# Two attention-and-Mamba layers with FP4 feed-forward on one core: four dA buffers, own rings for the C products, a thinner SP queue

## The chip, the cores and the metric

The program runs on one core of one Trainium2 chip. The metric is the time of one execution on the device in microseconds (us); lower is better.

## The reference

Input x is (8, 1024, 256). Layer 0 is attention with relative positions (16 heads of 16, so 8 x 16 = 128 heads of 1024 tokens), layer 1 two Mamba layers; each is followed by a gated feed-forward on blockwise FP4 values, and all are modulated by scales and shifts made from a condition. What matters here, cut down:

```python
# attention, per head: c2p and p2c are gathered diagonally from tables of relative positions
scores = (Q K^T) * scale + c2p + p2c ; probs = softmax(scores) ; ctx = probs V
# Mamba layer, per batch; D_INNER = 512, D_STATE = 16
u  = silu(conv(xc)) ; dt = softplus(x_dbl[:RANK] @ dt_w.T + dt_b) ; A = -exp(A_log)
dA = exp(dt_t[:, :, None] * A)
h  = dA * h + (dt_t * u_t)[:, :, None] * B_t[:, None, :]     # a scan over time
y  = einsum('bdn,bn->bd', h, C_t)
y  = (y + u * Dskip) * silu(z) ; h = y @ out_w.T
x  = layer_norm(h) * ln_w + ln_b + residual
```

## The kernel before, in words

Everything is written out by hand: each engine has its own program, and semaphores tie them. Stages follow each other: modulation, attention, its output product, feed-forward, two Mamba layers (`mamba_layer`, names mb_), feed-forward. The change touches two of them.

**Attention** (`attention_loop`, from L701). A loop over 128 heads, two per turn; per head 8 tiles of 128 queries (index i). For each tile TensorE makes scores one tile ahead (L866) and adds into them, by a transposing product, a 3-block band of position terms from `skew` (L870); two position tables of the next head (`table`, L883); turns the probabilities (L899); and makes the context of the tile before (L918). VectorE adds the other band (L1018) and takes the maximum (L1020), ScalarE makes the exponentials (L971) and keeps the tables in SBUF (L966). A table reaches its skewed form through DRAM: SP stores it (`store_table`, L784, one DMA per table, 16 per head), and loads it back with a row pitch one shorter (`load_skew`, L793, four DMAs for each of four parts of two tiles). SP works its queue in order: `head` (L796) waits until the head before has done its scores, loads the next head's three operands (L771), then the two operands of the tables of the head after (L775, tile `eopnd`), then for each i two stores, at certain i the loads of a part (each waits until its tables have landed), the values (L778) and the context store (L816). Part 3 of a head (tiles 6 and 7) is loaded in the next turn of `head`, at i = 0. TensorE needs it before the scores of tile 5.

**Mamba** (`mamba_layer`). 16 items per layer (8 batches, two halves of 512 time steps each, index t.u; the second half starts its scans from `carry`). Channels are on partitions in 4 chunks, and with 16 states an item has 64 slots s. In a slot:

- ScalarE makes dA[s] = exp(dt * A) (L2198) into a ring of DA_RING = 2 banks in PSUM;
- GpSimd makes bx[s] = dtu * B (L1921) into a ring of 4 in SBUF;
- VectorE scans (L2016) dA[s] and bx[s] into `hs` (PSUM, two banks) or, if GpSimd multiplies by C, into `hs_sb` (SBUF, two);
- the product with C: VectorE (L1976), one slot later, or GpSimd (L1928), three slots later, for the 18 slots of TIMES_C_POOL; both into one ring g of 4;
- TensorE sums the products over the states into y_ps (L2159), one slot later, in the order of slots.

```python
                        nc.vector.tensor_tensor_scan(state(s), dA[:, s % DA_RING, :], bx[:, s % RINGS, :],
```

The work of the neighbouring items is laid into the slots by tables of slot numbers (the AT_ names, L1590 on): input projections, convolution, the softplus of dt (ScalarE L2177 to L2184, VectorE L2002 on v and lnp, GpSimd L1934, L1937, L1940), gating (L1983), output projection, and the norm: statistics L1987 and L1993, reciprocal root on GpSimd (L1905 to L1910), centering on ScalarE (L2188), weight and shift on VectorE (L2040, L2044), residual on GpSimd (L1952). Layer 1 also adds a base row and a gate on VectorE (L2049, L2053). SP loads B and C rows, spread over all partitions, by quarters.

Of the kernel before, what the change touches and what calls it, by code (L numbers as in the profile page):

```python
# [2333 lines left out]
```

## Time and profile before

| | |
|---|---|
| median of 3 runs | 10254.26 us (10250.23 to 10259.6) |
| the profiled execution's own time | 10262.97 us |
| its span, first to last instruction | 10261.3 us |
| busy: TensorE (PE), VectorE (DVE) | 8391.0 us (82%), 8398.0 us (82%) |
| busy: ScalarE (ACT), GpSimd (POOL) | 5633.4 us (55%), 4948.9 us (48%) |
| mean granted TensorE clock | 0.923 of full speed |
| DMA | 1498.79 MB, mean 146 GB/s |

Busy times are sums over the whole span, so an engine that is full in one stage and idle in another shows a middling share. In a group of instructions, "x" is the count, then come busy time, mean ns of one, and the idle time of the engine just before them with what ended it. A duration includes any time in which the instruction is held back after it started. In a timeline, equal instructions that follow each other are one row ("x3"), with their time together.

### The profile page before, as it was taken

How to read it: one execution, taken by the hardware profiler on the slowest of the kernel's cores; microseconds unless marked ns; L12 is line 12 of the kernel's file. 1: busy time of each engine (PE TensorE's matmuls, PEld its weight loads, DVE VectorE, ACT ScalarE, POOL GpSimd, SP SyncE). 2: the span in 40 equal slices, each digit the busy share in tenths (PEclk: the TensorE clock that was granted, in tenths of full speed). 3: DMA queues.
4: the chain of work that ended last, by engine and by line, in shares of the span. 5: the costliest groups of instructions: out<-in, count | busy, mean ns of one | idle time of the engine just before them, and what ended most of it. 6: DMA issues, size and time to landing. Idle time of an engine off the chain costs nothing. (4 is left out here: it accounts for less than half of the span.)

```text
span 10261.3 us, 177062 instructions
## 1 busy us (share of the span) xinstructions
PE 8391.0 (82%) x48396; PEld 4841.9 (47%) x48396; DVE 8398.0 (82%) x13204; ACT 5633.4 (55%) x9153; POOL 4948.9 (48%) x4685
## 2 busy tenths in 40 slices
PE   4569899989988888499688888888688888887599
PEld 2236666666666666366333333333233333333366
DVE  4558888888888887699588888888688888888799
ACT  1237777777777776133365555555455555555233
POOL 0000000000000000088488888888598888888487
PEclk7779999999999999699898998898899999999799
DMA  5578888888888888311111111111122221122111
GB/s 178 204 234 281 277 278 279 279 279 278 277 279 277 277 278 261 111 43 42 61 74 76 76 68 55 68 74 75 51 80 84 84 84 71 62 81 80 45 43 40
DMA packets 1218155, 1498.79 MB, mean 146 GB/s; under 512 B 101997, under 2 KB 1073277, under 8 KB 1185000
## 3 DMA queue, kind: packets, MB, share of 16 engines
q1 hardware_dynamic: 1217832, 1495.78, 44.7%
q14 instruction: 279, 2.29, 0.1%
q8 instruction: 44, 0.72, 0.0%
HBM read 932.33 MB, written 564.60 MB: 146 GB/s over the span
## 5 line engine op out<-in xcount | busy, mean ns | idle before, releaser
L2159 PE MATMUL mb_y_ps<-mb_g,ident 128*128 128x512 f32 x4096 | 2227.9, 654 | 589.9 <-DVE mb_g L1976 356.3
L1921 POOL TENSOR_TENSOR mb_bx<-mb_dtu,mb_bc 128x512 f32<-128x512 f32 x2048 | 2569.3, 1282 | 132.7 <-DVE mb_hs L2016 78.6
L2198 ACT ACTIVATE mb_dA<-mb_dt,mb_a_neg 128x512 f32<-128x512 f32 x2048 | 1403.7, 689 | 1854.9 <-DVE mb_hs L2016 1181.4
L1355 POOL MEMSET f_magic<- 128x1 f32 x2 | 0.2, 98 | 3842.8 <-POOLq L127 3842.8
L2159 PEld LDWEIGHTS mb_y_ps<-mb_g,ident 128*128 128x128 f32 x4096 | 789.3, 204 | 1782.9 <-issue 755.4
L966 ACT ACTIVATE at_tab<-at_e_ps 128x384 f32<-128x384 f32 x2064 | 1011.8, 490 | 968.4 <-PE at_e_ps L883 967.4
L1020 DVE TENSOR_REDUCE at_nmax<-at_s_ps 128x1 f32<-128x1024 f32 x1025 | 1255.2, 1225 | 35.2
L899 PE MATMUL at_pT_ps<-ident,at_probs 128*128 128x128 f32 x8192 | 1115.7, 280 | 140.3 <-ACT at_probs L971 131.8
L971 ACT ACTIVATE at_probs<-at_s_ps,at_nmax 128x1024 f32<-128x1024 f32 x1025 | 1140.6, 1113 | 96.2 <-DVE at_nmax L1020 77.0
L899 PEld LDWEIGHTS at_pT_ps<-ident,at_probs 128*128 128x128 f32 x8192 | 920.0, 142 | 403.3 <-ACT at_probs L971 378.1
L2016 DVE TENSOR_TENSOR_SCAN mb_hs<-mb_dA,mb_carry,mb_bx 128x512 f32<-128x512 f32 x736 | 927.7, 1280 | 204.8 <-POOL mb_bx L1921 117.2
L1976 DVE TENSOR_TENSOR mb_g<-mb_hs,mb_bc 128x512 f32<-128x512 f32 x1472 | 994.0, 675 | 69.9 <-PE mb_y_ps L2159 68.6
L2016 DVE TENSOR_TENSOR_SCAN mb_hs<-mb_dA,mb_bx 128x512 f32<-128x512 f32 x736 | 893.6, 1223 | 165.0 <-ACT mb_dA L2198 96.1
L866 PE MATMUL at_s_ps<-at_opnd 105*128 105x512 bf16 (+3 forms) x2818 | 808.8, 327 | 201.9 <-DMA at_skew<-at_tables 199.2
L1018 DVE TENSOR_TENSOR at_s_ps<-at_s_ps,at_skew 128x384 f32<-128x384 f32 (+1 forms) x1025 | 541.2, 528 | 495.6 <-PE at_s_ps L870 375.1
L1928 POOL TENSOR_TENSOR mb_g<-mb_hs_sb,mb_bc 128x512 f32<-128x512 f32 x576 | 736.5, 1279 | 312.6 <-DVE mb_hs_sb L2016 180.2
L1025 DVE COPY at_probsT<-at_pT_ps 128x512 f32<-128x512 f32 x1024 | 697.0, 681 | 0.0
L918 PE MATMUL at_c_ps<-at_probsT,at_val 128*32 128x128 f32 x16384 | 663.9, 280 | 1.6 <-ACT at_probsT L978 1.6
L870 PE MATMUL at_s_ps<-ident,at_skew 128*128 128x128 f32 x2818 | 612.9, 275 | 0.0
L2092 PE MATMUL mb_ring<-mb_xc,mb_diag 128*128 128x512 f32 x1024 | 526.8, 600 | 41.6 <-ACT mb_u L2249 39.0
L918 PEld LDWEIGHTS at_c_ps<-at_probsT,at_val 128*32 128x32 f32 x16384 | 387.4, 109 | 214.6 <-issue 203.9
L866 PEld LDWEIGHTS at_s_ps<-at_opnd 105*128 105x128 bf16 x2818 | 242.8, 98 | 435.2 <-DMA at_skew<-at_tables 223.9
(236 smaller groups left out, 14473.1 us busy)
## 6 DMA issues: line engine op xcount, KB each, us to landing
at_tables<-at_tab SPq DMA_DIRECT2D x2064, 192.0 KB, 3.5
at_skew<-at_tables SPq DMA_DIRECT2D x1030, 256.0 KB, 3.1
mb_bc<-mb_bc_rows SPq DMA_DIRECT2D x256, 1024.0 KB, 6.4
at_skew<-at_tables SPq DMA_DIRECT2D x773, 128.0 KB, 3.5
at_opnd<-at_q_st SPq DMA_DIRECT2D x129, 210.0 KB, 3.4
at_opnd<-at_kl_st SPq DMA_DIRECT2D x129, 210.0 KB, 3.9
at_opnd<-at_kr_st SPq DMA_DIRECT2D x129, 210.0 KB, 5.2
at_eopnd<-at_q_st SPq DMA_DIRECT2D x130, 192.0 KB, 4.3
```

The lines of the kernel that those rows point to most:

```text
L866: mm = nc.tensor.matmul(s_ps[:, b, a * P:z * P], opnd[:, u, 0, q], opnd[:, u, side, a * P:z * P], start=True, stop=(len(near) == 0))
L899: mm = nc.tensor.transpose(pT_ps[:, hb, k * P:(k + 1) * P], probs[:, i % 2, c:c + P], ident[:, :])
L918: mm = nc.tensor.matmul(c_ps[lane * VW:(lane + 1) * VW, q:q + P], val[:, h.u, k + lane, :], probsT[:, i0 % 2, (k + lane) * P:(k + lane + 1 ...
L966: nc.scalar.activation(tab[:, e, :], e_ps[:, 0:BAND], ACT.Copy).then_inc(s_tab, 1)
L971: nc.scalar.activation(probs[:, i % 2, :], s_ps[:, i % 2, :], ACT.Exp, bias=nmax[:, i % 2:i % 2 + 1], scale=1.0).then_inc(s_exp, 1)
L1020: nc.vector.tensor_reduce(nmax[:, b:b + 1], s_ps[:, b, :], axis=AX.X, op=ALU.max, negate=True).then_inc(s_max, 1)
L1921: pool.tensor_tensor(bx[:, s % RINGS, :], dtu[:, c, :], bc[:, 0, n, :], ALU.mult).then_inc(s_bx, 1)
L1928: pool.tensor_tensor(g[:, s1 % RINGS, :], state(s1), bc[:, 1, s1 % STATE, :], ALU.mult).then_inc(s_gp, 1)
L1976: nc.vector.tensor_tensor(g[:, s1 % RINGS, :], state(s1), bc[:, 1, n, :], ALU.mult).then_inc(s_g, 1)
L2016: nc.vector.tensor_tensor_scan(state(s), dA[:, s % DA_RING, :], bx[:, s % RINGS, :], initial=carry[:, s:s + 1] if k.u else 0.0, op0=ALU.mu ...
L2159: nc.tensor.matmul(y_ps[:, c % 2, :], ident[:, :], g[:, s1 % RINGS, :], start=False, stop=(n == STATE - 1)).then_inc(s_y, 1)
L2198: nc.scalar.activation(dA[:, s % DA_RING, :], dt[:, c, :], ACT.Exp, scale=a_neg[:, c, n:n + 1]).then_inc(s_dA, 1)
```

## The change

In attention: `eopnd` and its loads are gone, the tables are made from the first 96 rows of `opnd`, which has a semaphore for each of its three parts. One DMA stores both tables of a tile. The operands of head n + 2 are loaded at i = 6, once the scores of head n are done; the loads of a part come ahead of the store of their i.

In Mamba: DA_RING is 4, of which two buffers are in PSUM (s % 4 in 0, 1) and two in SBUF, `dA_sb` (s % 4 in 2, 3). The ring g becomes g_dve (3) and g_pool (2), each freed by TensorE's sum of the slot that used it; TensorE sums GpSimd's products 5 slots after their scan, VectorE's 1 slot after. GpSimd makes 14 C products in place of 18, and applies the output norm's weight and shift (two sums and products over 128 x 1024) in VectorE's place. The softplus steps work in dt and dtu in place of v, e and lnp, ScalarE's in two slots, GpSimd's three in three slots. Centering is done in two halves in two slots. SP waits only for the bx products before it loads B rows, and for the sums before C rows. Some slot numbers move.

The core of the diff:

```diff
-            def store_table(n1, u1, e):
-                ge(sp, s_tab, n1 * NE + e + 1)
-                part = e // 2 // (TT // len(PARTS))
-                sp.dma_start(table_dram[u1, e % 2, e // 2, 0:P, SPAN:SPAN + BAND], tab[:, e, :]).then_inc(s_tw[part], 16)
+            def store_tables(n1, u1, t):
+                ge(sp, s_tab, n1 * NE + 2 * t + 2)
+                part = [t < z for _, z in PARTS].index(True)
+                sp.dma_start(table_dram[u1, :, t, 0:P, SPAN:SPAN + BAND].rearrange("s p u -> p s u"),
+                             tab[:, 2 * t:2 * t + 2, :]).then_inc(s_tw[part], 16)
...
-                load_opnd(n + 1, 1 - u)
-                ge(sp, s_E, (n + 1) * NE)
-                load_eopnd(n + 2, u)
                 for i in range(TT):
-                    for e in range(2 * i, 2 * i + 2):
-                        store_table(n + 1, 1 - u, e)
                     for part, (_, z) in enumerate(PARTS):
-                        if z - 1 + LAG - 1 == i + 1:
+                        if z + 1 == i:
                             load_skew(n + 1, 1 - u, part)
-                        if z - 1 + LAG - 1 == i + 1 + TT:
+                        if z + 1 == i + TT:
                             load_skew(n, u, part)
-                    if i == 0:
+                    if i == TT - 2:
+                        ge(sp, s_S, n * TT + TT)
+                        load_opnd(n + 2, u)
+                    store_tables(n + 1, 1 - u, i)
+                    if i == 2:
...
-                mm = nc.tensor.matmul(e_ps[:, 0:BAND], eopnd[:, u1, side, t * P:(t + 1) * P],
+                mm = nc.tensor.matmul(e_ps[:, 0:BAND], opnd[0:ROWS, u1, side, t * P:(t + 1) * P],
...
-AT_DTK, AT_DTK_ACT = (52, 2, 15, 32), (58, 8, 21, 38)
-AT_DTK_DVE, AT_DTK_POOL = (59, 9, 22, 39), (63, 13, 26, 43)
+AT_DTK, AT_DTK_ACT = (52, 2, 15, 32), (56, 8, 21, 38)
+AT_DTK_DVE, AT_DTK_POOL = (58, 11, 23, 40), (59, 12, 24, 41)
 AT_Z, AT_Z_ACT = (40, 43, 54, 56), (46, 49, 60, 62)
 AT_U = 45
 AT_SILU_Z = 12
 AT_XDBL, AT_XDBL_ACT = 47, 53
-AT_Y = (29, 38, 54, 4)
-AT_ONORM = 26
-AT_RES = 44
-AT_OCENTER, AT_OSCALE = 34, 37
-AT_HCENTER, AT_HSCALE = 56, 59
-AT_XIN = 48
-AT_LN = 50
+AT_Y = (29, 38, 54, 7)
+AT_ONORM, AT_OCENTER, AT_OAFFINE, AT_OGATE = 26, (33, 34), (36, 38), 44
+AT_RES, AT_RES_LAST = 43, 48
+AT_XIN = 50
+AT_LN, AT_HCENTER, AT_HSCALE = 53, (58, 59), 61
 RINGS = 4
-DA_RING = 2
-
-TIMES_C_POOL = tuple(s for s in range(IC * STATE) if s * 18 // (IC * STATE) != (s + 1) * 18 // (IC * STATE))
+DA_RING, DA_PSUM = 4, 2
+G_DVE, G_POOL = 3, 2
+
+TIMES_C_POOL = tuple(s for s in range(IC * STATE) if s * 14 // (IC * STATE) != (s + 1) * 14 // (IC * STATE))
 POOL_LAG = 3
+SUM_LAG_POOL = 5
...
-        g = sb("g", [P, RINGS, BANK])
+        g_dve = sb("g_dve", [P, G_DVE, BANK])
+        g_pool = sb("g_pool", [P, G_POOL, BANK])
+        dA_sb = sb("dA_sb", [P, DA_RING - DA_PSUM, BANK])
         carry = sb("carry", [P, SLOTS])
         yz = sb("yz", [P, IC, BANK])
         o_sb = sb("o_sb", [P, QT, D])
         hs_sb = sb("hs_sb", [P, 2, BANK])
-        dA = pb("dA", [P, DA_RING, BANK])
+        dA = pb("dA", [P, DA_PSUM, BANK])
...
+        def decay(s):
+            i = s % DA_RING
+            return dA[:, i, :] if i < DA_PSUM else dA_sb[:, i - DA_PSUM, :]
...
+        def product_read(eng, t, slots, i, ring):
+
+            i = turned_over(i, ring, len(slots))
+            if i >= 0 or t.n_static != 0:
+                t = t if i >= 0 else t.plus(-1)
+                ge(eng, s_y, summed(t, slots[i]))
...
-                            sp.wait_ge(s_y, k.n * SLOTS + (IC - 1) * STATE + n + 4)
                         for i in range(2):
+                            if i == 1 and not first_body(k):
+                                at = (IC - 1) * STATE + n
+                                sp.wait_ge(s_y, summed(k, max(range(at, at + 4), key=sum_order)))
...
-                            m1 = t.n * SLOTS + s1
-                            pool.wait_ge(s_scan, m1 + 1)
-                            ge(pool, s_y, m1 - RINGS + 1)
-                            pool.tensor_tensor(g[:, s1 % RINGS, :], state(s1), bc[:, 1, s1 % STATE, :],
+                            p = slots_before(s1, True)
+                            pool.wait_ge(s_scan, t.n * SLOTS + s1 + 1)
+                            product_read(pool, t, by_pool, p, G_POOL)
+                            pool.tensor_tensor(g_pool[:, p % G_POOL, :], state(s1), bc[:, 1, s1 % STATE, :],
                                                ALU.mult).then_inc(s_gp, 1)
...
+                    if tail and s == AT_OAFFINE[0]:
+                        t = k.plus(-1)
+                        pool.wait_ge(s_ocen, t.n * 2 + 2)
+                        pool.tensor_tensor(o_sb[:, :, :], o_sb[:, :, :], ln[:, 0:1, :].to_broadcast([P, QT, D]),
+                                           ALU.mult).then_inc(s_oaff, 1)
+                    if tail and s == AT_OAFFINE[1]:
+                        pool.wait_ge(s_oaff, k.plus(-1).n * 2 + 1)
+                        pool.tensor_tensor(o_sb[:, :, :], o_sb[:, :, :], ln[:, 1:2, :].to_broadcast([P, QT, D]),
+                                           ALU.add).then_inc(s_oaff, 1)
...
-                    ge(dve, s_y, m - RINGS + 1)
-                    nc.vector.tensor_tensor(g[:, s1 % RINGS, :], state(s1), bc[:, 1, n, :], ALU.mult).then_inc(s_g, 1)
+                    d = slots_before(s1, False)
+                    product_read(dve, t, by_dve, d, G_DVE)
+                    nc.vector.tensor_tensor(g_dve[:, d % G_DVE, :], state(s1), bc[:, 1, n, :], ALU.mult).then_inc(s_g, 1)
...
-                        nc.vector.tensor_tensor_scan(state(s), dA[:, s % DA_RING, :], bx[:, s % RINGS, :],
+                        nc.vector.tensor_tensor_scan(state(s), decay(s), bx[:, s % RINGS, :],
...
-                        if s == AT_OSCALE:
-                            dve.wait_ge(s_ocen, b.n + 1)
-                            nc.vector.tensor_tensor(o_sb[:, :, :], o_sb[:, :, :],
-                                                    ln[:, 0:1, :].to_broadcast([P, QT, D]), ALU.mult).then_inc(s_ochain, 1)
-                        if s == AT_OSCALE + 1:
-                            dve.wait_ge(s_ochain, done + 3)
-                            nc.vector.tensor_tensor(o_sb[:, :, :], o_sb[:, :, :],
-                                                    ln[:, 1:2, :].to_broadcast([P, QT, D]), ALU.add).then_inc(s_ochain, 1)
...
+                    if s >= SUM_LAG_POOL and scan or s < SUM_LAG_POOL and tail:
+                        lag = s - SUM_LAG_POOL
+                        t, s1 = (k, lag) if lag >= 0 else (b, SLOTS + lag)
...
-                        nc.scalar.activation(dA[:, s % DA_RING, :], dt[:, c, :], ACT.Exp,
+                        nc.scalar.activation(decay(s), dt[:, c, :], ACT.Exp,
```

What the diff does not show is how the instructions stand. SP's queue in attention, the end of one head and the start of the next, before:

```order
L793 DMA at_skew<-at_tables 128x2x256 x2
L793 DMA at_skew<-at_tables 128x2x128 x2
L784 DMA at_tables<-at_tab 128x384 x2
L771 DMA at_opnd<-at_q_st 105x1024
L771 DMA at_opnd<-at_kl_st 105x1024
L771 DMA at_opnd<-at_kr_st 105x1024
L775 DMA at_eopnd<-at_q_st 96x1024
L775 DMA at_eopnd<-at_kl_st 96x1024
L784 DMA at_tables<-at_tab 128x384 x2
L793 DMA at_skew<-at_tables 128x2x256 x2
L793 DMA at_skew<-at_tables 128x2x128
L793 DMA at_skew<-at_tables 128x128
```

and in the change:

```order
L778 DMA at_tables<-at_tab 128x2x384
L768 DMA at_opnd<-at_q_st 105x1024
L768 DMA at_opnd<-at_kl_st 105x1024
L768 DMA at_opnd<-at_kr_st 105x1024
L778 DMA at_tables<-at_tab 128x2x384
L788 DMA at_skew<-at_tables 128x2x256 x2
L788 DMA at_skew<-at_tables 128x2x128 x2
L778 DMA at_tables<-at_tab 128x2x384 x2
L788 DMA at_skew<-at_tables 128x2x256 x2
L788 DMA at_skew<-at_tables 128x2x128
L788 DMA at_skew<-at_tables 128x128
L778 DMA at_tables<-at_tab 128x2x384 x2
```

The five operand loads between tables and tables are gone from the start of the head; three of them stand between part 1 and the last tables.

VectorE in Mamba, a stretch of four to five slots in the first half of a batch, before (a scan is printed as SCALAR_TENSOR_TENSOR):

```order
L2016 SCALAR_TENSOR_TENSOR mb_hs<-mb_dA,mb_bx 128x512
L1973 COPY mb_carry<-mb_hs 128x1
L1976 TENSOR_TENSOR mb_g<-mb_hs,mb_bc 128x512
L2016 SCALAR_TENSOR_TENSOR mb_hs<-mb_dA,mb_bx 128x512
L1973 COPY mb_carry<-mb_hs 128x1
L1976 TENSOR_TENSOR mb_g<-mb_hs,mb_bc 128x512
L2016 SCALAR_TENSOR_TENSOR mb_hs_sb<-mb_dA,mb_bx 128x512
L1973 COPY mb_carry<-mb_hs 128x1
L1976 TENSOR_TENSOR mb_g<-mb_hs,mb_bc 128x512
L2016 SCALAR_TENSOR_TENSOR mb_hs<-mb_dA,mb_bx 128x512
L1973 COPY mb_carry<-mb_hs_sb 128x1
```

and in the change:

```order
L2076 SCALAR_TENSOR_TENSOR mb_hs_sb<-mb_dA,mb_bx 128x512
L2032 COPY mb_carry<-mb_hs 128x1
L2036 TENSOR_TENSOR mb_g_dve<-mb_hs,mb_bc 128x512
L2076 SCALAR_TENSOR_TENSOR mb_hs<-mb_dA_sb,mb_bx 128x512
L2032 COPY mb_carry<-mb_hs_sb 128x1
L2076 SCALAR_TENSOR_TENSOR mb_hs<-mb_dA_sb,mb_bx 128x512
L2032 COPY mb_carry<-mb_hs 128x1
L2036 TENSOR_TENSOR mb_g_dve<-mb_hs,mb_bc 128x512
L2076 SCALAR_TENSOR_TENSOR mb_hs<-mb_dA,mb_bx 128x512
L2032 COPY mb_carry<-mb_hs 128x1
L2036 TENSOR_TENSOR mb_g_dve<-mb_hs,mb_bc 128x512
```

The scans read `mb_dA` (PSUM) in two slots and `mb_dA_sb` (SBUF) in the next two; `mb_bx` is in SBUF throughout. All else is as before in these slots.

## Rows read from the trace of the kernel before

**Rows 1.** busy time by engine in three stretches (attention, Mamba layer 0, layer 1)
```profile
core 0: us, PE busy (x) PEld busy (x) DVE busy (x) ACT busy (x) POOL busy (x), PEclk, DMA share, GB/s
1000.00:3800.00 2800.00, 2522.00 (x28194) 1853.34 (x28193) 2280.36 (x3368) 1991.44 (x3156) 0.00 (x0) 0.99 0.88 278
5500.00:6900.00 1400.00, 1169.65 (x2577) 497.25 (x2576) 1243.49 (x1727) 819.66 (x1285) 1234.55 (x1034) 0.90 0.18 69
8000.00:9400.00 1400.00, 1151.99 (x2589) 490.51 (x2587) 1234.20 (x1653) 797.27 (x1245) 1243.16 (x1002) 0.93 0.22 79
```

**Rows 2.** SP's stores and skew loads, 1000 to 3800 us; duration ns min/median/max
```profile
L784 SPq DMA_DIRECT2D at_tables<-at_tab x1684: 319/373/637, 1002.7 to 3799.7; - x188
...
L793 SPq DMA_DIRECT2D at_skew<-at_tables x1684: 370/469/1152, 1000.7 to 3797.6; - x188
```

**Rows 3.** waits of all engines, 1000 to 3800 us; in total, times, longest
```profile
PE at_s_ps L866 <- DMA at_skew<-at_tables: 159.5, 118, 2.5
```

**Rows 4.** timeline of TensorE in attention; start, duration, idle time before
```profile
2003.31 0.45 PE L866 MATMUL at_s_ps<-at_opnd 105*128 105x512 bf16 x2 [1.72 <-DMA at_skew<-at_tables]
```

**Rows 5.** timeline of SP's queue at the end of one head
```profile
2016.50 1.91 SPq L793 DMA_DIRECT2D at_skew<-at_tables  x4
...
2019.62 0.36 SPq L771 DMA_DIRECT2D at_opnd<-at_q_st  x1
...
2022.28 0.84 SPq L784 DMA_DIRECT2D at_tables<-at_tab  x2
...
2023.17 2.44 SPq L793 DMA_DIRECT2D at_skew<-at_tables  x4
```

**Rows 6.** waits of SP's queue, 1000 to 3800 us
```profile
SPq L793 <- DMA at_tables<-at_tab: 671.5, 316, 3.7
...
SPq L784 <- ACT at_tab L966: 91.4, 321, 0.5
```

**Rows 7.** instruction groups in Mamba, 5500 to 6900 us (x650: 8000 to 9400 us)
```profile
L1921 POOL TENSOR_TENSOR mb_bx<-mb_dtu,mb_bc 128x512 f32<-128x512 f32 x642 | 805.7, 1282 | 45.2 <-issue 22.6 <-DVE mb_hs L2016 21.0 <-POOL mb_dtu L1940 1.2
...
L1921 POOL TENSOR_TENSOR mb_bx<-mb_dtu,mb_bc 128x512 f32<-128x512 f32 x650 | 817.9, 1285 | 56.7 <-DVE mb_hs L2016 32.2 <-issue 23.0 <-POOL mb_dtu L1940 1.2
...
L2016 DVE TENSOR_TENSOR_SCAN mb_hs<-mb_dA,mb_carry,mb_bx 128x512 f32<-128x512 f32 x233 | 294.3, 1281 | 72.8 <-POOL mb_bx L1921 42.8 <-ACT mb_dA L2198 28.9
...
L2016 DVE TENSOR_TENSOR_SCAN mb_hs<-mb_dA,mb_bx 128x512 f32<-128x512 f32 x230 | 279.5, 1223 | 52.6 <-ACT mb_dA L2198 31.9 <-POOL mb_bx L1921 19.8
...
L1976 DVE TENSOR_TENSOR mb_g<-mb_hs,mb_bc 128x512 f32<-128x512 f32 x462 | 312.1, 676 | 22.7 <-PE mb_y_ps L2159 22.0
...
L1952 POOL TENSOR_TENSOR mb_o_sb<-mb_o_sb,mb_xin 128x1024 f32<-128x1024 f32 x10 | 23.6, 2358 | 0.0
```

**Rows 8.** timeline of VectorE in Mamba layer 0
```profile
6226.86 4.84 DVE L2040 TENSOR_TENSOR mb_o_sb<-mb_o_sb,mb_ln 128x1024 f32<-128x1024 f32 x1
...
6234.00 1.27 DVE L2044 TENSOR_TENSOR mb_o_sb<-mb_o_sb,mb_ln 128x1024 f32<-128x1024 f32 x1
```

**Rows 9.** timeline of GpSimd in the same microseconds
```profile
6226.89 3.72 POOL L1921 TENSOR_TENSOR mb_bx<-mb_dtu,mb_bc 128x512 f32<-128x512 f32 x3
...
6232.91 1.27 POOL L1921 TENSOR_TENSOR mb_bx<-mb_dtu,mb_bc 128x512 f32<-128x512 f32 x1 [2.31 <-DVE mb_hs L2016]
```

**Rows 10.** timeline of VectorE in Mamba layer 1
```profile
9083.71 1.21 DVE L2053 TENSOR_TENSOR mb_o_sb<-mb_o_sb,mb_mod 128x1024 f32<-128x1024 f32 x1
```

**Rows 11.** timeline of GpSimd in the same microseconds
```profile
9083.81 2.23 POOL L1937 TENSOR_TENSOR mb_dt<-mb_v,mb_e 128x512 f32<-128x512 f32 x1
```

**Rows 12.** all executions of L2002; duration ns min/median/max
```profile
L2002 DVE SCALAR_TENSOR_TENSOR mb_v<-mb_v,mb_lnp x128: 672/1323/3625, 5041.1 to 9491.7; 128x512 f32<-128x512 f32 x128
```

**Rows 13.** DMA issues, 1000 to 3800 us; last column us to landing
```profile
at_opnd<-at_kl_st SPq DMA_DIRECT2D x105, 210.0 KB, 3.9
```

**Rows 14.** waits of all engines in Mamba, 5500 to 6900 us
```profile
POOL mb_g L1928 <- PE mb_y_ps L2159: 43.2, 21, 2.8
...
DVE mb_hs L2016 <- ACT mb_dA L2198: 60.8, 38, 2.6
```

More of the change, by code:

```diff
@@ L837, in _ @@
                 ge(sp, s_ctx[u], 16 * (heads // 2))
-            ge(sp, s_op[0], 48 * (heads // 2 + 1))
+            for k in range(3):
+                for u in range(2):
+                    ge(sp, s_op[k][u], 16 * (heads // 2 + 1))
             ge(sp, s_val[0], 16 * (heads // 2 + 1))
-            for u in range(2):
-                ge(sp, s_eop[u], 32 * (heads // 2 + 1))
+            for part, (a, z) in enumerate(PARTS):
+                ge(sp, s_tw[part], 16 * (z - a) * (heads + 1))
             for part in range(len(PARTS)):
@@ L1619, with sum_order, sums_to, last_summed @@
 TC_DVE, TC_POOL = slots_before(IC * STATE, False), slots_before(IC * STATE, True)
+def sum_order(s):
+    return (s + (SUM_LAG_POOL if s in TIMES_C_POOL else 1), s in TIMES_C_POOL)
+def sums_to(s, first=False, last=False):
+    at, pool = sum_order(s)
+    n = 0
+    for i in range(IC * STATE):
+        i_at, i_pool = sum_order(i)
+        n += (i_at, i_pool) <= (at, pool)
+        if not first:
+            n -= (i_at - IC * STATE, i_pool) > (at, pool)
+        if not last:
+            n += (i_at + IC * STATE, i_pool) <= (at, pool)
+    return n
+def last_summed(c):
+    return max(range(c * STATE, (c + 1) * STATE), key=sum_order)
+def turned_over(i, ring, count):
+    return i - ring if i >= ring else max(range(i % ring, count, ring)) - count
 EXP_LN = "natural_log_exp_and_others"
@@ L1769, in mamba_layer @@
         s_dA, s_bx, s_scan, s_g, s_y = (sem(n) for n in ("dA", "bx", "scan", "g", "y"))
-        s_gp = sem("g_pool")
+        s_gp = sem("g_from_pool")
         s_z, s_zc, s_sz = sem("z"), sem("z_kept"), sem("sz_done")
         s_yz, s_rest = sem("y_gated"), sem("rest_done")
-        s_o, s_oc, s_ochain, s_ors = (sem(n) for n in ("out", "out_kept", "ochain", "o_rstd"))
+        s_o, s_oc, s_ochain, s_ors, s_oaff = (sem(n) for n in ("out", "out_kept", "ochain", "o_rstd", "o_affine"))
         s_res, s_st = sem("res"), sem("stored")
         HSTEPS = 3
-        OSTEPS = 4 if not last else 6
+        OSTEPS = 2 if not last else 4
         s_rows = s_hrow if first else s_src
@@ L1900, in _ @@
             pool.wait_ge(s_set, 6)
+            pool.wait_ge(s_const, 16 * 2)
             def norm_scale(t, side, done):
@@ L1957, in body @@
                         norm_scale(t, 0, s_hrs)
-                    if head and s == AT_DTK_POOL[0]:
-                        make_dtu(k.plus(1), 0)
             run(pool, body)
@@ L2261, in body @@
                     if head and s == AT_DTK_ACT[0]:
-                        log_steps(a, 0, 1)
-                    if tail and s == AT_OCENTER:
+                        exp_steps(a, 0, 1)
+                    if head and s == AT_DTK_ACT[0] + 1:
+                        log_steps(a, 0)
+                    if tail and s in AT_OCENTER:
+                        half = AT_OCENTER.index(s)
                         act.wait_ge(s_ors, b.n + 1)
-                        center(o_sb, 1).then_inc(s_ocen, 1)
-                    if ahead and first and s == AT_HCENTER:
-                        t = k.plus(2)
+                        center(o_sb, 1, half).then_inc(s_ocen, 1)
+                    if ahead and first and s in AT_HCENTER:
+                        t, half = k.plus(2), AT_HCENTER.index(s)
                         act.wait_ge(s_hrs, t.n + 1)
-                        center(src, 0).then_inc(s_hcen, 1)
+                        center(src, 0, half).then_inc(s_hcen, 1)
             run(act, body)
```

122 lines of the change are left out of this document (67 added, 55 removed).

## The prediction

> **What bounds the kernel now.** The busy shares over the whole span (VectorE 82%, GpSimd 48%) are averages over stages, so I cut the span into stretches first. There are three kinds of work [rows 1]: attention (some 3400 us; GpSimd idle, DMA share 0.88), the two Mamba layers (some 4500 us; VectorE and GpSimd both about 88% busy) and two feed-forward stages that the change leaves alone.
>
> *Attention.* In 2800 us the sync engine SP issued 1684 skew loads, 16 per head, so 105 heads at 26.6 us each [rows 2]; there are 128 heads. Once per head TensorE stands still for a skew load: 159.5 us over these 105 heads, 1.5 us each [rows 3]. The stall has one place: 1.72 us before the scores of tile 5 [rows 4], which wait for part 3 of the skews. That part is issued late: the timeline of SP shows, one behind the other, the last loads of part 2, the stores of tile 7, the five operand loads, the stores of tile 0, and only then the four loads of part 3 [rows 5]. SP is the engine that sets this. It issues 39 DMAs per head (16 stores, 16 skews, 5 operand loads, values, context); four in a row take 1.91 us [rows 5], 0.47 each, hence 18.3 us. Its waits are 6.4 us for its own stores to land and 0.9 us for ScalarE [rows 6]: 25.6 of 26.6 us. SP hardly waits for anybody but itself.
>
> *Mamba.* An item is 64 slots; GpSimd made 642 and 650 of the bx products in two stretches of 1400 us, so one item takes 139.6 us in layer 0 and 137.8 in layer 1, mean 138.7, and there are 32 items [rows 7]. GpSimd is busy 122.7 us of an item (1234.55 over 10.03 items and 1243.16 over 10.16 [rows 1]) and VectorE as long (1243.49 and 1234.20); each is idle 16 us. Neither bounds alone: they wait for each other over rings of four and two.
>
> **A thing in the rows that matters most.** L2040 and L2044 are the same kind of VectorE instruction on the same shape, both operands in SBUF. One took 4.84 us, the other 1.27 us [rows 8]. GpSimd, in the same microseconds, ran three products during the first, from 6226.89 to 6230.61, then waited; VectorE's instruction ended 1.1 us after that. During the second GpSimd was idle but for the end of an earlier product [rows 9]. So a VectorE instruction with two SBUF operands and a GpSimd product shut each other out. It works the other way as well: L2053 ran its normal 1.21 us at 9083.71 [rows 10], and the GpSimd product that started 0.1 us later took 2.23 us in place of 1.27 [rows 11], 0.97 us lost. The shutting out costs GpSimd about the VectorE duration less 0.24. L2002, also with two SBUF operands, takes 0.67 us at best, 1.32 at the median and up to 3.6 [rows 12]. All scans of the kernel before read dA from PSUM and one operand from SBUF, and they stay at 1.22 and 1.28 us beside a busy GpSimd [rows 7]. In the order of instructions shown with the change, a scan has the very form of L2002, SCALAR_TENSOR_TENSOR.
>
> **The change, part by part.**
>
> 1. *Attention queue.* One store per tile instead of two, the two loads of the tables' operand gone, the other three moved from the head's start to before the store of tile 6. SP then issues 8+16+3+2 = 29 DMAs, 13.6 us by 0.47. A store now has 256 rows in place of 128; skew loads of 256 rows take 469 ns at the median and stores of 128 take 373 [rows 2], so size hardly counts. SP comes in step with ScalarE, and part 3 goes out earlier in the head by at least the 2.7 us from the first of the five loads to the stores behind them [rows 5], more than the stall, which goes. What is late next: TensorE's own loop with VectorE (TensorE 90% busy [rows 1]), so a little may come back. Bounds: nothing, and 1.5 us x 128 = 195 us. I take 1.3 us, 170 us off, nearer the stall's row. The moved operand load has two tiles (some 6 us) until it is read, and lands in 3.9 us at the median [rows 13]. DMA traffic per head is 278 GB/s by 26.6 us, 7.4 MB, and falls by 0.39 MB, in proportion about as much as the period, so the share stays at 0.88.
>
> 2. *Four C products per item from GpSimd to VectorE.* GpSimd -4 x 1.23 = -4.9 us (1.23 is the pitch of products in a row: 3.72 us for three [rows 9]); VectorE +4 x 0.68 = +2.7 [rows 7].
>
> 3. *Output norm's weight and shift from VectorE to GpSimd.* VectorE -4.8 -1.3 = -6.1 us [rows 8]; GpSimd +2 x 2.36 = +4.7, by its sum of the same shape [rows 7]. Points 2 and 3 leave GpSimd at 122.5 and VectorE at 119.3 us per item.
>
> 4. *Own product rings, sums of GpSimd's products two slots and more later, B rows loaded without waiting for C's reader.* These remove waits: GpSimd's for TensorE's sum, 4.3 us per item [rows 14], and some of VectorE's for the same. They add no instruction. The softplus steps, spread over slots and made in dt and dtu, are as many as before: nothing, hidden as before by the scans around them.
>
> 5. *Four dA buffers, two of them in SBUF.* VectorE's wait for dA, 6.1 us per item [rows 14], goes. But half the scans, 32 per item, now read dA and bx both from SBUF. No row shows such a scan. Bounds: no exclusion at all, 0; or the whole scan. By L2053, nearest in kind, each costs GpSimd 1.25 - 0.24 = 1.0 us: 32.6 us per item. I take this. It cannot hide: GpSimd has 122.5 us of its own work, so 155 us is the floor of an item. To it I add half of today's idle time, 8 us, since the waits for scans stay: **163 us**, +24.4 against 138.7. Check from VectorE's side: 119.3 us of work leave 44 us, 1.4 us of waiting per such scan, one GpSimd product: it fits.
>
> The Trainium skill, "SBUF — State Buffer", section "Who interferes with whom", states this rule: a VectorE instruction with two SBUF inputs contends with a GpSimd instruction that reads SBUF, and whoever starts first holds the pair for the whole instruction. By that rule the loss would be the full 1.25 us, 40 us per item, and the total some 240 us more than mine; the trace agrees with the exclusion and puts 0.97 on an instruction of 1.21.
>
> **Sum.** Against the profiled execution's 10262.97 us: 32 x 24.4 = +781, -170: 10874. The median of the three runs is 9 us lower: **10865 us**. (0.2%, 20 us, is about what a measurement of this kernel can tell from no change.)
>
> **Rivals.**
> A. *The scan with two SBUF operands does not shut GpSimd out* (faster). For: it streams slowly (1.22 us for 512 elements, where a plain product takes 0.68), so it might leave room; it has no row. Against: L2002's form. Then an item is GpSimd's 122.5 plus 8 us, 131: -7.7 x 32 = -246, -170: 9840 us. It decides wherever dA_sb scans stay near 1.25 us. Chance 0.15.
> B. *Exclusion as forecast, but attention gains nothing*, because another wait on a DMA takes the stall's place (the operand load is now only two tiles ahead). 11035 us. Chance 0.15.
> C. *VectorE loses turn after turn*, as L2040 did three times: GpSimd runs to the end of its ring of four, stands idle through the scan, and its other work (122.5 less 64 x 1.23, 44 us) hides worse beside the scans that leave it room. Item 175: +1162, -170: 11245 us. Chance 0.12.
> D. *The exclusion is short or mostly fits into GpSimd's 16 idle us*, and attention's gain pays for it: item 144, +170 -170: 10255 us. Chance 0.02.
> My forecast: 0.56.
>
> **Range.** Low: an item at the floor of 155, and all of attention's 195: +522 -195, about 10575; a little below it, 10540. High: C, 11245, to 11270. That holds the forecast, B and C, 0.83 of the chance less what their spread loses. Faster: A and a trifle of D, 0.16; the same 0.01; slower 0.83.
>
> **What the changed profile would show.** Scans on mb_dA_sb at about 2 to 2.6 us, those on mb_dA at 1.22 and 1.28; bx products on GpSimd with a mean of 1.5 to 1.7 us in place of 1.28, items of about 163 us; ScalarE waiting more, VectorE no longer waiting for mb_dA. In attention no wait of TensorE for at_skew, and heads of 25.3 us. I am wrong if dA_sb scans take 1.25 us (A), if heads stay at 26.6 us (B), or if items come out under 155 us, which the floor forbids as long as each such scan costs GpSimd 1 us.

## The result and the profile after

The changed kernel took 10568.72 us in the median of four runs (10565.74 to 10570.99), the kernel before 10252.24 us on the same chip (10246.74 to 10259.6): a ratio of 1.0308 (95% interval 1.029 to 1.0326), 316 us slower. The profiled execution took 10568.0 us, with a span of 10566.3 us (before: 10261.3).

Where the 305 us between the two spans arise can be read from two kinds of rows, each with all executions of a line (duration ns min/median/max, then first and last start): the maximum of attention, one per tile and one more, and the scans. The kernel before:

```profile
L1020 DVE TENSOR_REDUCE at_nmax<-at_s_ps x1025: 1223/1225/1226, 661.2 to 4066.7; 128x1 f32<-128x1024 f32 x171
...
L2016 DVE TENSOR_TENSOR_SCAN mb_hs<-mb_dA,mb_bx x736: 1195/1222/1232, 5047.9 to 9402.5; 128x512 f32<-128x512 f32 x184
L2016 DVE TENSOR_TENSOR_SCAN mb_hs<-mb_dA,mb_carry,mb_bx x736: 1255/1281/1294, 5177.9 to 9533.9; 128x512 f32<-128x512 f32 x184
```

and the changed kernel, whose scans read dA from PSUM (mb_dA) or from SBUF (mb_dA_sb):

```profile
L1015 DVE TENSOR_REDUCE at_nmax<-at_s_ps x1025: 1223/1225/1226, 662.8 to 3854.2; 128x1 f32<-128x1024 f32 x171
...
L2076 DVE TENSOR_TENSOR_SCAN mb_hs<-mb_dA,mb_bx x416: 1190/1218/1232, 4830.1 to 9685.4; 128x512 f32<-128x512 f32 x139
...
L2076 DVE TENSOR_TENSOR_SCAN mb_hs<-mb_dA_sb,mb_bx x384: 1190/2180/3292, 4833.2 to 9688.2; 128x512 f32<-128x512 f32 x192
L2076 DVE TENSOR_TENSOR_SCAN mb_hs<-mb_dA_sb,mb_carry,mb_bx x384: 1249/2130/3294, 4980.2 to 9838.5; 128x512 f32<-128x512 f32 x192
```

Attention ran from 661.2 to 4066.7 us before, 26.6 us per head, and runs from 662.8 to 3854.2 us now, 24.93 per head: **214 us less**. The scans ran from 5047.9 to 9533.9 us before (4486.0 us) and run from 4830.1 to 9838.5 us (5008.4 us): **522 us more**, 16.3 us for each of the 32 items. The rest is the same to 3 us.

The stretches that answer to [rows 1]:

```profile
core 0: us, PE busy (x) PEld busy (x) DVE busy (x) ACT busy (x) POOL busy (x), PEclk, DMA share, GB/s
1000.00:3800.00 2800.00, 2702.33 (x30136) 1953.36 (x30138) 2444.66 (x3598) 2114.00 (x3374) 0.00 (x0) 1.00 0.89 281
5500.00:6900.00 1400.00, 1107.80 (x2304) 441.54 (x2302) 1294.90 (x1573) 736.73 (x1153) 1371.73 (x910) 0.87 0.17 63
8000.00:9400.00 1400.00, 1125.36 (x2334) 448.77 (x2335) 1299.30 (x1531) 718.26 (x1116) 1368.61 (x885) 0.89 0.20 72
```

**Attention.** TensorE is busy for 97% of the first stretch (2702.33 of 2800 us), before 90%. It no longer stands still for the skews: the 159.5 us of [rows 3] have become this (waits in the same stretch; total, times, longest):

```profile
PE at_e_ps L878 <- DMA at_opnd<-at_q_st: 7.3, 12, 1.0
PEld at_s_ps L861 <- DMA at_skew<-at_tables: 1.0, 5, 0.2
...
SPq L788 <- DMA at_tables<-at_tab: 763.7, 435, 4.2
SPq L778 <- ACT at_tab L961: 336.4, 391, 2.1
```

SP has time in hand now: it waits 336.4 us for ScalarE's tables, where it waited 91.4 [rows 6]. Its queue at the end of a head shows why (to be held against [rows 5]): operand loads, the tables of tile 6, part 2, and then the tables of tile 7 and of the next head's tile 0 and part 3 with no load between.

```profile
2007.04 0.37 SPq L768 DMA_DIRECT2D at_opnd<-at_q_st  x1
2007.50 0.59 SPq L768 DMA_DIRECT2D at_opnd<-at_kl_st  x1
2008.18 0.43 SPq L768 DMA_DIRECT2D at_opnd<-at_kr_st  x1
2008.72 0.40 SPq L778 DMA_DIRECT2D at_tables<-at_tab  x1
2010.68 1.96 SPq L788 DMA_DIRECT2D at_skew<-at_tables  x4
2012.75 1.42 SPq L778 DMA_DIRECT2D at_tables<-at_tab  x2
2018.52 1.90 SPq L788 DMA_DIRECT2D at_skew<-at_tables  x4
```

**Mamba.** GpSimd is busy for 98% of both stretches (1371.73 and 1368.61 of 1400 us), before 88%, though by the forecast's count its own work stayed the same (122.5 us per item for 122.7). The groups that answer to [rows 7], 5500 to 6900 us:

```profile
L1966 POOL TENSOR_TENSOR mb_bx<-mb_dtu,mb_bc 128x512 f32<-128x512 f32 x577 | 919.1, 1615 | 0.0
...
L2076 DVE TENSOR_TENSOR_SCAN mb_hs<-mb_dA_sb,mb_bx 128x512 f32<-128x512 f32 x110 | 216.8, 1974 | 19.7 <-POOL mb_bx L1966 19.0
...
L2076 DVE TENSOR_TENSOR_SCAN mb_hs<-mb_dA,mb_carry,mb_bx 128x512 f32<-128x512 f32 x115 | 146.3, 1280 | 26.1 <-POOL mb_bx L1966 24.7
L2076 DVE TENSOR_TENSOR_SCAN mb_hs<-mb_dA,mb_bx 128x512 f32<-128x512 f32 x119 | 144.6, 1221 | 30.4 <-POOL mb_bx L1966 29.4
...
L1978 POOL TENSOR_TENSOR mb_dtu<-mb_q,mb_dtu 128x512 f32<-128x512 f32 x36 | 70.5, 1958 | 0.0
...
L2000 POOL TENSOR_TENSOR mb_o_sb<-mb_o_sb,mb_ln 128x1024 f32<-128x1024 f32 x9 | 29.6, 3286 | 0.0
L2014 POOL TENSOR_TENSOR mb_o_sb<-mb_o_sb,mb_xin 128x1024 f32<-128x1024 f32 x9 | 29.4, 3271 | 0.0
```

577 products in 1400 us are an item in 1400 / 577 x 64 = 155.3 us. A scan whose dA is in PSUM takes what it took before, 1221 and 1280 ns; one whose dA is in SBUF takes 1974, and up to 3294. GpSimd's bx product has gone from 1282 to 1615 ns and has no idle time before it. The shutting out can be watched. VectorE:

```profile
6098.58 2.21 DVE L2076 TENSOR_TENSOR_SCAN mb_hs<-mb_dA_sb,mb_bx 128x512 f32<-128x512 f32 x1 [1.10 <-POOL mb_bx L1966]
...
6101.46 1.23 DVE L2076 TENSOR_TENSOR_SCAN mb_hs<-mb_dA,mb_bx 128x512 f32<-128x512 f32 x1
```

and GpSimd:

```profile
6096.29 3.40 POOL L1966 TENSOR_TENSOR mb_bx<-mb_dtu,mb_bc 128x512 f32<-128x512 f32 x2
6099.65 2.19 POOL L1973 TENSOR_TENSOR mb_g_pool<-mb_hs_sb,mb_bc 128x512 f32<-128x512 f32 x1
6101.81 1.26 POOL L1966 TENSOR_TENSOR mb_bx<-mb_dtu,mb_bc 128x512 f32<-128x512 f32 x1
```

The scan starts at 6098.58 beside a running bx product that ends about 6099.7, and ends 1.1 us after that, at 6100.79. GpSimd's next product starts at 6099.65 and ends at 6101.84, again 1.05 us after the scan's end: 2.19 us where the one behind it takes 1.26. Each engine loses about a microsecond.

### The profile page after: what moved, and what is told of

The parts are those of the page before. It is cut to its first block and busy times, and to the rows that moved or that the text cites. A ratio compares the mean times of both kernels' runs of the same rounds, so it can differ in the third digit from the quotient of the medians.

```text
span 10566.3 us, 174069 instructions
## 1 busy us (share of the span) xinstructions
PE 8669.1 (82%) x48396; PEld 4813.3 (46%) x48396; DVE 9045.9 (86%) x13268; ACT 5626.0 (53%) x9153; POOL 5864.0 (55%) x4621
## 5 line engine op out<-in xcount | busy, mean ns | idle before, releaser
L1966 POOL TENSOR_TENSOR mb_bx<-mb_dtu,mb_bc 128x512 f32<-128x512 f32 x2048 | 3291.5, 1630 | 13.3 <-DVE mb_hs L2076 13.0
L2210 PE MATMUL mb_y_ps<-mb_g_dve,ident 128*128 128x512 f32 x3200 | 1976.9, 710 | 1008.0 <-DVE mb_g_dve L2036 1003.1
L2210 PEld LDWEIGHTS mb_y_ps<-mb_g_dve,ident 128*128 128x128 f32 x3200 | 579.7, 209 | 2179.4 <-DVE mb_g_dve L2036 1952.2
L2265 ACT ACTIVATE mb_dA_sb<-mb_dt,mb_a_neg 128x512 f32<-128x512 f32 x1024 | 733.1, 719 | 1345.8 <-DVE mb_hs L2076 943.9
L2265 ACT ACTIVATE mb_dA<-mb_dt,mb_a_neg 128x512 f32<-128x512 f32 x1024 | 705.3, 689 | 955.7 <-DVE mb_hs L2076 692.6
L2036 DVE TENSOR_TENSOR mb_g_dve<-mb_hs,mb_bc 128x512 f32<-128x512 f32 x1600 | 1073.5, 671 | 0.5 <-PE mb_y_ps L2210 0.5
L2076 DVE TENSOR_TENSOR_SCAN mb_hs<-mb_dA_sb,mb_carry,mb_bx 128x512 f32<-128x512 f32 x384 | 762.7, 1993 | 70.7 <-POOL mb_bx L1966 65.2
L2076 DVE TENSOR_TENSOR_SCAN mb_hs<-mb_dA_sb,mb_bx 128x512 f32<-128x512 f32 x384 | 757.5, 1976 | 69.0 <-POOL mb_bx L1966 64.5
L1973 POOL TENSOR_TENSOR mb_g_pool<-mb_hs_sb,mb_bc 128x512 f32<-128x512 f32 x448 | 667.9, 1491 | 12.3 <-DVE mb_hs_sb L2076 10.5
L2076 DVE TENSOR_TENSOR_SCAN mb_hs<-mb_dA,mb_carry,mb_bx 128x512 f32<-128x512 f32 x416 | 528.6, 1279 | 98.2 <-POOL mb_bx L1966 74.0
```

Source lines behind the costliest of these rows:

```text
L1966: pool.tensor_tensor(bx[:, s % RINGS, :], dtu[:, c, :], bc[:, 0, n, :], ALU.mult).then_inc(s_bx, 1)
L1973: pool.tensor_tensor(g_pool[:, p % G_POOL, :], state(s1), bc[:, 1, s1 % STATE, :], ALU.mult).then_inc(s_gp, 1)
L2036: nc.vector.tensor_tensor(g_dve[:, d % G_DVE, :], state(s1), bc[:, 1, n, :], ALU.mult).then_inc(s_g, 1)
L2076: nc.vector.tensor_tensor_scan(state(s), decay(s), bx[:, s % RINGS, :], initial=carry[:, s:s + 1] if k.u else 0.0, op0=ALU.mult, op1=ALU.a ...
L2210: nc.tensor.matmul(y_ps[:, c % 2, :], ident[:, :], g_dve[:, d % G_DVE, :], start=False, stop=(s1 == last_summed(c))).then_inc(s_y, 1)
L2265: nc.scalar.activation(decay(s), dt[:, c, :], ACT.Exp, scale=a_neg[:, c, n:n + 1]).then_inc(s_dA, 1)
```

## The experiments

Two theories stood at the start. The first is that of the prediction: half of the scans take turns with GpSimd. The second puts the loss on the rest of the rewrite of Mamba: work moved to GpSimd, rings, slots, the loads of the B and C rows. Each run's expectations say what either asks for, in numbers.

### Where dA lies

**All dA in PSUM** again, a ring of two, and the rest of the change left as it is.

```diff
-DA_RING, DA_PSUM = 4, 2
+DA_RING, DA_PSUM = 2, 2
```

> The changed kernel with two dA buffers, both in PSUM; all else of the change stays. Theory 1 (shutting out): no scan has two SBUF operands, so each of the 32 scans per item gives back about 1.0 us of GpSimd time; items of 155 us fall to 124 to 131, the total to 9580 to 9850 us, and bx products on GpSimd come back from 1630 ns to about 1290. Theory 2 (the moved slots, the later sums or GpSimd's two norm operations cost the time): they are all still there, and a ring of two holds the scan nearer to ScalarE: 10570 us or more.

Measured: 9933.51 us, ratio 0.9712 (0.9696 to 0.9729) to the kernel before on its chip (10228.37 us). The second theory falls: nothing was lost in the rest of the rewrite. With one line of constants the change goes from 3.1% slower to 2.9% faster. The line changes both the place of dA and the depth of its ring; the third run below parts them.

```profile
5500.00:6900.00 1400.00, 1189.24 (x2613) 500.14 (x2612) 1254.61 (x1775) 835.57 (x1312) 1270.48 (x1037) 0.91 0.19 72
...
L1965 POOL TENSOR_TENSOR mb_bx<-mb_dtu,mb_bc 128x512 f32<-128x512 f32 x660 | 839.4, 1294 | 45.5 <-DMA mb_bc<-mb_bc_rows 43.7 <-DVE mb_hs L2075 1.4
L1977 POOL TENSOR_TENSOR mb_dtu<-mb_q,mb_dtu 128x512 f32<-128x512 f32 x41 | 54.1, 1320 | 21.0 <-ACT mb_p L2250 21.0
L1999 POOL TENSOR_TENSOR mb_o_sb<-mb_o_sb,mb_ln 128x1024 f32<-128x1024 f32 x10 | 23.5, 2351 | 0.0
```

Every kind of GpSimd product is short again (1294, 1320, 2351 in place of 1615, 1958, 3286 ns), so it was not the new work that was slow, but everything on GpSimd. The item is 1400 / 660 x 64 = 135.8 us, not the 124 to 131 expected, and the time lies above the 9580 to 9850 expected: GpSimd is busy for 123.2 us of the item (1270.48 over 10.31 items), as forecast, but idle for 12.6.

**All dA in SBUF**, a ring of two, so that all 64 scans have two operands in SBUF.

```diff
-DA_RING, DA_PSUM = 4, 2
+DA_RING, DA_PSUM = 2, 0
```

> The changed kernel with two dA buffers, both in SBUF: all 64 scans of an item have two SBUF operands. Theory 1: GpSimd's 122 us of an item and 64 scans at 1.0 us each cannot overlap: items of 187 to 195 us, 11580 to 11850 us in all. Theory 2: dA's place does not matter: as e1 within 1%.

Measured: 11477.7 us, ratio 1.1224 (1.1201 to 1.1246), a little under the range.

```profile
5500.00:6900.00 1400.00, 997.56 (x1958) 396.68 (x1959) 1252.62 (x1337) 634.71 (x976) 1384.51 (x768) 0.83 0.14 55
...
L1965 POOL TENSOR_TENSOR mb_bx<-mb_dtu,mb_bc 128x512 f32<-128x512 f32 x490 | 913.1, 1885 | 10.1 <-DMA mb_bc<-mb_bc_rows 7.9 <-DVE mb_hs_sb L2075 2.2
L2075 DVE TENSOR_TENSOR_SCAN mb_hs<-mb_dA_sb,mb_bx 128x512 f32<-128x512 f32 x200 | 379.5, 1907 | 62.2 <-POOL mb_bx L1965 61.1
```

**One buffer in PSUM, one in SBUF**: the change's 32 scans, with the ring of two of the kernel before. It parts the place of dA from the number of buffers.

```diff
-DA_RING, DA_PSUM = 4, 2
+DA_RING, DA_PSUM = 2, 1
```

> The changed kernel with two dA buffers, one in PSUM and one in SBUF: 32 scans per item with two SBUF operands as in the changed kernel, but a ring of two. Tells what the two more buffers are worth. Theory 1: GpSimd's floor of 155 us holds as before, since it and not ScalarE bounds: 10570 to 10700 us. If the ring's depth matters on its own, over 10750.

Measured: 10606.35 us, ratio 1.0374 (1.0357 to 1.0391), within the expectation. Against the change's 1.0308 the two further buffers are worth 0.7%, some 70 us; by the spans of the profiled executions, 10601.2 and 10566.3 us on two chips, 35 us. Against the first experiment, on the same chip, DA_PSUM alone differs: with one of the two buffers in SBUF the kernel is 3.7% slower than the kernel before, with both in PSUM 2.9% faster.

```profile
5500.00:6900.00 1400.00, 1098.24 (x2274) 447.23 (x2273) 1266.47 (x1564) 732.23 (x1140) 1356.79 (x903) 0.86 0.16 63
...
L1966 POOL TENSOR_TENSOR mb_bx<-mb_dtu,mb_bc 128x512 f32<-128x512 f32 x573 | 857.0, 1518 | 17.3 <-DMA mb_bc<-mb_bc_rows 15.2 <-DVE mb_hs_sb L2076 2.2
```

Together these are a series in one quantity. Per item of the layer-0 stretch (1400 us by the products in it, 64 to an item):

| scans with dA in SBUF | span, us | item, us | GpSimd busy | GpSimd idle |
|---|---|---|---|---|
| 0 | 9934.1 | 135.8 | 123.2 | 12.6 |
| 32 | 10601.2 | 156.4 | 151.5 | 4.8 |
| 32, ring of four (the change) | 10566.3 | 155.3 | 152.1 | 3.1 |
| 64 | 11477.7 | 182.9 | 180.8 | 2.0 |

GpSimd's busy time grows by 28.3 us for the first 32 scans and 29.3 for the next: **0.9 us for each scan**, over the whole range. Some of it is first taken out of the idle time, which is why the first 32 scans cost 667 us and the next 877.

### Attention

**The kernel before with the new attention alone.**

```diff
-def attention_loop ...   (of the kernel before)
+def attention_loop ...   (of the change, with store_tables, opnd in three parts and the new place of the loads)
```

> The kernel before with the attention part of the change alone. Theory 1: heads of 24.9 us in place of 26.6, which is 128 x 1.67 = 214 us off: 10040 us. Rival: attention's gain hangs on nothing that Mamba does, so any other value would mean that the stages are not separate; 10150 or more would refute the sum.

Measured: 10033.73 us, ratio 0.9813 (0.9797 to 0.983), 195 us faster; its heads take 24.89 us (659.3 to 3844.7 us). Of the 2.9% that the first experiment gained on the same chip, 1.9% are attention's, and the other 1.0%, 100 us, are left for Mamba with dA in PSUM. Its scans agree: they run over 4377.8 us there (4824.5 to 9202.3), 108 us less than in the kernel before.

**The same, with two stores per tile again.** It parts the number of DMAs from the place of the operand loads.

```diff
-                ge(sp, s_tab, n1 * NE + 2 * t + 2)
-                sp.dma_start(table_dram[u1, :, t, 0:P, SPAN:SPAN + BAND].rearrange("s p u -> p s u"),
-                             tab[:, 2 * t:2 * t + 2, :]).then_inc(s_tw[part], 16)
+                for side in range(2):
+                    ge(sp, s_tab, n1 * NE + 2 * t + side + 1)
+                    sp.dma_start(table_dram[u1, side, t, 0:P, SPAN:SPAN + BAND],
+                                 tab[:, 2 * t + side, :]).then_inc(s_tw[part], 16)
```

> The kernel before with the attention part of the change (as e4), but two stores per tile as before, so SP issues 37 DMAs per head instead of 29. If the number of issues is what held SP back, 8 x 0.47 = 3.8 us per head come back to its queue and part of the stall with them: 10070 us or more. If the five operand loads at the head's start were the cause, nothing returns: 10034 us within 20.

Measured: 10051.48 us, ratio 0.9806 (0.979 to 0.9823). Against the 0.9813 of the run before, on another chip, nothing comes back that can be told from zero. By the trace's own clock the heads take 25.05 us (664.6 to 3871.3 us) in place of 24.89, 21 us in all.

**The kernel before with one store per tile and nothing else**, the operand loads still at the head's start.

```diff
-                    for e in range(2 * i, 2 * i + 2):
-                        store_table(n + 1, 1 - u, e)
+                    store_tables(n + 1, 1 - u, i)
```

> The kernel before, with one single edit: SP stores both tables of a tile with one DMA (8 stores per head in place of 16); the operand loads stay at the head's start. Theory 1, what carried attention's gain is where the operand loads stand, not how many DMAs SP issues: SP's order is the same at the start of a head, so little is gained, ratio 0.990 to 1.000 (0 to 100 us). Theory 2, SP's issue time per head is the bound (39 DMAs by 0.47 us and 6.4 us of landings, 25.6 of 26.6 us): eight DMAs fewer take 3 us out of SP's head and the whole gain of the new queue appears here as well, ratio 0.981 to 0.984.

Measured: 10219.8 us, ratio 0.9969 (0.9958 to 0.9981), as the first theory asked. The stall stays (waits, 1000 to 3800 us), against 159.5 us in [rows 3]:

```profile
PE at_s_ps L866 <- DMA at_skew<-at_tables: 132.7, 113, 2.2
...
SPq L794 <- DMA at_tables<-at_tab: 1034.1, 395, 5.0
```

Eight DMAs fewer per head bring 0.37 us of the 1.7 (heads of 26.23 us, 660.0 to 4017.8). What SP saves in issuing it waits longer for its stores to land, 1034.1 us for 671.5 [rows 6]. By these three runs most of the gain comes from what stands ahead of part 3 in SP's queue. Moving three operand loads, dropping two and giving each part of `opnd` a semaphore of its own were not tried apart.

### The rest of Mamba, with dA in PSUM

All four runs start from the first experiment (ratio 0.9712).

**Weight and shift back on VectorE.** The two `pool.tensor_tensor` at AT_OAFFINE become `nc.vector.tensor_tensor` in the same slots.

> As e1 (changed kernel, dA in two PSUM banks), with the output norm's weight and shift back on VectorE. Theory: they take 1.1 us each on VectorE plus what GpSimd's products hold them back (3.7 us in the kernel before), against 4.7 us on GpSimd: items 2 to 5 us longer, 9990 to 10090 us. Rival: GpSimd bounds e1, and its 4.7 us relief counts: below 9900.

Measured: 9934.96 us, ratio 0.9695 (0.9679 to 0.9711): no difference, and 55 us under the lowest time expected.

```profile
5500.00:6900.00 1400.00, 1186.13 (x2613) 497.35 (x2614) 1273.40 (x1792) 833.79 (x1306) 1234.20 (x1015) 0.92 0.19 72
...
L1965 POOL TENSOR_TENSOR mb_bx<-mb_dtu,mb_bc 128x512 f32<-128x512 f32 x658 | 838.9, 1300 | 63.1 <-DMA mb_bc<-mb_bc_rows 47.2 <-DVE mb_hs L2067 15.5
```

Over 10.28 items (658 products) VectorE has 123.9 us of work and GpSimd 120.0, in place of 121.7 and 123.2. Both stay at least 12 us below the item, and the item stays at 136.2 us. Here each engine has more idle time than the work that is shifted, and shifting it does nothing.

**18 C products on GpSimd** in place of 14, as many as before the change.

```diff
-TIMES_C_POOL = tuple(s for s in range(IC * STATE) if s * 14 // (IC * STATE) != (s + 1) * 14 // (IC * STATE))
+TIMES_C_POOL = tuple(s for s in range(IC * STATE) if s * 18 // (IC * STATE) != (s + 1) * 18 // (IC * STATE))
```

> As e1, with 18 C products on GpSimd instead of 14. GpSimd gets 4.9 us more per item, VectorE 2.7 less. GpSimd is busy 91% and VectorE 90% in e1. If GpSimd is the tighter of the two: up to 4.9 us per item more, 10000 to 10090 us. If VectorE is: 9930 or less.

Measured: 9908.67 us, ratio 0.9667 (0.9651 to 0.9683). This is the fastest kernel of the study, 3.3% under the kernel before.

```profile
5500.00:6900.00 1400.00, 1179.90 (x2654) 502.13 (x2655) 1266.51 (x1755) 842.98 (x1326) 1339.81 (x1092) 0.93 0.19 71
...
L1965 POOL TENSOR_TENSOR mb_bx<-mb_dtu,mb_bc 128x512 f32<-128x512 f32 x668 | 862.1, 1316 | 17.0 <-DMA mb_bc<-mb_bc_rows 16.6 <-DVE mb_hs L2075 0.4
```

The item is 134.1 us, GpSimd is busy for 128.4 of it and idle for 5.8. That VectorE was the tighter engine is not shown: its busy time hardly moved (121.3 us). Beside the run before, which is on the same chip, the gain is 26 us.

**22 C products on GpSimd**, the same edit with 22.

> The change with two PSUM dA buffers, 22 of the 64 C products on GpSimd in place of 14 (18 gave ratio 0.9667 to the kernel before, 14 gave 0.9712). Theory 1, VectorE is the tighter engine of an item and GpSimd has slack while it waits: four more products off VectorE, 2.7 us of an item's work, give another 10 to 30 us, ratio 0.964 to 0.966. Theory 2, the two engines are balanced at 18: GpSimd gets 4 x 1.23 = 4.9 us more per item, 132 us of own work, and that is now the bound of an item of 134.5 us: ratio 0.967 to 0.980, up to 150 us slower than with 18.

Measured: 10454.91 us, ratio 1.0198 (1.0181 to 1.0215), about 545 us slower than with 18. Both theories were wrong: the second expected a loss, but at most 150 us, and no engine's own work became the bound. GpSimd's busy time is 134.5 us of an item of 154.0 (582 products in the stretch), 19.5 us idle, and its waits in the same stretch show where the idle time goes:

```profile
DVE mb_hs L2075 <- POOL mb_bx L1965: 272.7, 155, 4.1
...
POOL mb_g_pool L1972 <- PE mb_y_ps L2217: 172.3, 93, 3.5
```

172.3 us over 9.1 items, 18.9 each, GpSimd stands before a C product until TensorE has summed the product two earlier, whose buffer it needs; with 18 products the same wait was 19.4 us in the whole stretch. TensorE sums GpSimd's product 5 slots after its scan, and the ring has two buffers. With 14 products the scan of a product comes 9 or 10 slots after that of the last but one, with 18 7 or 8, with 22 5 or 6, hardly more than the 5. VectorE then waits for bx behind it. The wait is measured; that the slots cause it is argued, and 22 products with a ring of three were not run.

**Semaphores of their own for B and C rows**, so that bx waits for the B rows alone.

```diff
-                            pool.wait_ge(s_bc[n // 4], k.n * 32 + 32)
+                            pool.wait_ge(s_bc[0][n // 4], k.n * 16 + 16)
```

> As e1, with a semaphore of its own for the B rows, so that GpSimd starts an item's bx products when B has landed and need not wait for C. In e1 GpSimd waits 4.4 us per item for these loads. If that wait sets the item's length, up to 4.4 us x 32 = 140 us off e1's 9934: 9790 to 9890. If it only takes the place of a wait for the scan, within 20 us of e1.

Measured: 9936.85 us, ratio 0.9698 (0.9682 to 0.9715): no difference. The wait went, and the time did not:

```profile
L1965 POOL TENSOR_TENSOR mb_bx<-mb_dtu,mb_bc 128x512 f32<-128x512 f32 x661 | 839.8, 1295 | 22.3 <-DVE mb_hs L2077 22.1
```

The expectation's second case held, within 20 us of the first experiment. GpSimd waited 43.7 us for the rows there; now it waits 22.1 us for room in bx's ring, and the rest is spread over its C products and the softplus steps (mb_g_pool 15.6 us where it was 2.9).

## Why the prediction was right, and where its sizes were off

The direction, the mechanism and the place were those forecast. The size was not: 316 us slower where 613 were forecast, with 10568.72 us near the low end of the range (10540). Point by point:

1. **Attention queue**: forecast 170 us, measured 214 by the heads and 195 by the run of attention alone (on another chip, where the kernel before, itself 24 us faster, has no profile). The step that failed is the size of the stall. [rows 3] give the wait of the matmul, 1.5 us per head; the weight load ahead of it waits for the same skew and longer, 1.76 us per head over the 105 heads, which the prediction did not read (waits of the kernel before, same stretch):

```profile
PEld at_s_ps L866 <- DMA at_skew<-at_tables: 184.4, 105, 2.8
```

   So the upper bound of 195 us was too low. And next to nothing came back, against "a little may come back": TensorE went to 97% busy, and 1.67 of those 1.76 us per head went. The argument on SP was half right. "Size hardly counts" held (a store of both tables takes 390 ns at the median, one of a single table took 373 [rows 2]), but the count of stores was worth only 0.37 us per head by itself and 0.16 within the new queue (25.05 and 24.89); the place and number of the operand loads carry the rest. Rival B, no gain in attention, has fallen: the moved operand loads cost TensorE 7.3 us in 2800.

2. **C products and the norm's weight and shift**: forecast to leave GpSimd 122.5 us of its own work, measured 123.2 with dA in PSUM. "VectorE at 119.3" measured 121.7. That the moves cost nothing was right; the runs with 18 products and with weight and shift on VectorE change the time by 0.5% and not at all.

3. **Rings**: GpSimd's wait for TensorE's sum went, and so did VectorE's for dA; in the changed kernel VectorE waits before its scans for bx (90.7 us in 1400). Forecast as gains that the other waits take up, and the first experiment puts a number on the whole of the new Mamba with dA in PSUM: an item of layer 0 goes from 139.6 to 135.8 us, and over both layers 108 us are gained, 3.4 per item. Rival A asked for 131 and would have been 9840 us; without the shutting out the kernel takes 9934.

4. **dA in SBUF**: forecast 32.6 us per item (its own 1.25 - 0.24, times 32, gives 32.3), measured 28.9, 0.90 us per scan for the 1.0 taken from one instruction [rows 10, 11]. The scans on `mb_dA_sb` take 1.94 to 1.97 us on average, just under the "2 to 2.6". The floor of 155 us, own work and shutting out together, is 152.1 us in the trace. The Trainium skill, "SBUF — State Buffer", "Who interferes with whom", has the first to start hold the pair for the whole instruction. The series agrees with the taking of turns and puts 0.90 us on scans that last 1.21 to 1.28 us alone, so by about 0.35 us less than the whole.

5. **The idle time on top of the floor** is the step that failed most. "Half of today's idle time, 8 us, since the waits for scans stay": GpSimd is idle for 3.1 us per item. The waits did not stay. As the scans take more of GpSimd's time, its idle time shrinks towards nothing: 12.6, 4.8 and 2.0 us in the last column of the table. Terms 4 and 5 were 3.7 and 4.9 us too large and own work 0.7 too small, 7.9 us of an item together: 163.1 - 7.9 = 155.2, where layer 0 measured 155.3. Over 32 items that is 253 of the 297 us by which the forecast was high; the other 44 are attention's. That the item landed on the "floor" of 155 is partly luck: the floor was 3 us lower, and 3 us of idle time stood on it.

Rival C, VectorE losing turn after turn, would have shown as an idle GpSimd, which is not there. The longest scans, up to 3.29 us, do not show it either: four of them between 5061 and 5529 us, like this one, stand behind one long GpSimd product of 2.3 us, not behind two turns.

```profile
5372.94 3.29 DVE L2076 TENSOR_TENSOR_SCAN mb_hs<-mb_dA_sb,mb_carry,mb_bx 128x512 f32<-128x512 f32 x1
...
5372.78 2.35 POOL L2004 TENSOR_TENSOR mb_o_sb<-mb_o_sb,mb_ln 128x1024 f32<-128x1024 f32 x1
```
